# Attention: the order of the three chains in a shared PSUM bank, with the features' chain begun in slot 5 of the batch ahead

## The reference, cut to what matters

```python
x = x + attn_b(layernorm(x), ...)
# attn_b:
q, k, v = split(x @ Wq), split(x @ Wk), split(x @ Wv)
q_amp, k_amp = amp_norm(q), amp_norm(k)   # a = softplus(t); a / sqrt(mean(a*a) + 1e-6)
q_phi, k_phi = pi * tanh(split(x @ Wqp)), pi * tanh(split(x @ Wkp))
scores_phase = (q_amp cos(q_phi)) . (k_amp cos(k_phi)) + (q_amp sin(q_phi)) . (k_amp sin(k_phi))
scores = scale * (q . k) + lam * scale * scores_phase
out = softmax(causal(scores)) @ v
return out.reshape(b, s, d) @ Wo
```

## Time and profile before

| | us |
|---|---|
| median of 3 executions | 1296.38 |
| lowest and highest | 1288.96, 1299.49 |
| profiled execution, its own time | 1298.49 |
| span of the profiled execution | 1296.7 |
| PE busy in the span | 1108.9 (86%) |
| DVE busy | 913.4 (70%) |
| ACT busy | 658.2 (51%) |
| mean granted clock of PE | 0.912 |

### The profile page before, as it was taken

The page is one execution under the profiler, slowest core; times in us unless marked ns, Lnnn a source line. Parts: engine busy times, 40 slices in busy tenths (PEclk is TensorE's granted clock), DMA queues, the critical chain, the costliest instruction groups (busy, mean ns, idle before and its releaser), DMA issues. The chain is left out here.

```text
span 1296.7 us, 16118 instructions
## 1 busy us (share of the span) xinstructions
PE 1108.9 (86%) x5200; PEld 655.8 (51%) x5200; DVE 913.4 (70%) x1933; ACT 658.2 (51%) x1204; POOL 261.1 (20%) x294
## 2 busy tenths in 40 slices
PE   4798888885999999786888888888979968999996
PEld 1222233322666667443455555555556636766774
DVE  2778888884878777675857677675775627787775
ACT  1233333443654555388356565665655646555553
POOL 1444444451000000030122122111212220000000
PEclk9888888886899999888688898998999988999999
DMA  5000000000242322246967568675756302312321
GB/s 189 0 1 1 0 0 0 1 1 1 66 131 66 98 99 66 37 142 169 307 166 203 133 175 204 166 199 136 204 136 148 76 27 105 130 67 81 117 66 65
DMA packets 45502, 129.04 MB, mean 100 GB/s; under 512 B 6512, under 2 KB 8560, under 8 KB 38768
## 3 DMA queue, kind: packets, MB, share of 16 engines
q1 hardware_dynamic: 43376, 127.53, 34.8%
q10 hardware_dynamic: 2048, 0.53, 0.2%
HBM read 88.72 MB, written 36.70 MB: 97 GB/s over the span
## 5 line engine op out<-in xcount | busy, mean ns | idle before, releaser
L1457 DVE TENSOR_REDUCE attn_maxima<-attn_ps_p 128x1 f32<-128x512 f32 (+3 forms) x235 | 146.0, 637 | 101.9 <-PE attn_ps_p L965 87.0
L1834 ACT ACTIVATE moe_hidden<-moe_ps_h 128x512 f32<-128x512 f32 x128 | 76.4, 597 | 147.3 <-PE moe_ps_y L1772 145.7
L1376 POOL TENSOR_SCALAR_AFFINE_SELECT attn_probs<-attn_probs 128x512 f32<-128x512 f32 x128 | 85.1, 700 | 319.0 <-ACT attn_probs L1209 319.0
L960 PE MATMUL attn_ps_p<-attn_stack 96*128 96x384 f32 (+3 forms) x341 | 121.3, 399 | 9.9 <-DVE attn_maxima L1457 9.0
L1956 DVE TENSOR_TENSOR moe_gated<-moe_ps_y,moe_gate_all 128x512 f32<-128x512 f32 x106 | 73.1, 690 | 75.6 <-issue 46.8
L1008 PE MATMUL attn_ps_q<-attn_stack 128*128 128x128 f32 (+3 forms) x343 | 109.7, 384 | 11.3 <-DMA attn_stack<-attn_neg_max 8.6
L1754 PE MATMUL moe_ps_h<-moe_x_high,moe_w_high 128*128 128x512 f32 x256 | 107.5, 420 | 0.0
L1457 DVE TENSOR_REDUCE attn_maxima<-attn_ps_t 128x1 f32<-128x384 f32 (+3 forms) x117 | 74.4, 636 | 45.6 <-PE attn_ps_t L965 43.6
L585 POOL TENSOR_TENSOR rwkv_rs<-rwkv_recept,rwkv_state 128x512 f32<-128x512 f32 x64 | 76.3, 1193 | 136.2 <-DVE rwkv_state L664 132.7
L1756 PE MATMUL moe_ps_h<-moe_x_high,moe_w_low 128*128 128x512 f32 x256 | 103.1, 403 | 0.0
L1755 PE MATMUL moe_ps_h<-moe_x_low,moe_w_high 128*128 128x512 f32 x256 | 102.8, 402 | 0.0
(11 more groups left out here) (256 smaller groups left out, 2452.0 us busy)
## 6 DMA issues: line engine op xcount, KB each, us to landing
moe_gate_all<-moe_gates SPq DMA_DIRECT2D x128, 256.0 KB, 4.9
attn_kept<-attn_parts SPq DMA_DIRECT2D x16, 1536.0 KB, 7.9
attn_stack<-attn_kept SPq DMA_DIRECT2D x64, 384.0 KB
attn_stack<-attn_kept SPq DMA_DIRECT2D x64, 192.0 KB
attn_value<-attn_values SPq DMA_DIRECT2D x5, 1792.0 KB, 12.0
attn_values<-attn_early SPq DMA_DIRECT2D x2, 1792.0 KB, 5.6
attn_values<-attn_probs SPq DMA_DIRECT2D x2, 1792.0 KB, 21.6
experts_in_w<-in_w SPq DMA_DIRECT2D x2, 1024.0 KB, 11.2
```

The costliest lines, as they stand in the source:

```text
L960: return mm(tiles(m)[:, i, :], stack[0][q][0:ROWS, h + i, t * P:(t + 1) * P], stack[1][q][0:ROWS, h + i, 0:(t + 1) * P], **flags)
L1376: nc.gpsimd.affine_select(out=tile, in_=tile, compare_op=ALU.is_ge, fill=0.0, base=0, pattern=[[0, 4], [1, P]], channel_multiplier=-1).the ...
L1457: nc.vector.tensor_reduce(maxima[:, u % 2, h:h + heads, t], tiles, AX_X, ALU.max).then_inc(g_free, 1)
```

## The change

Five things are moved; no instruction of the loop is added or taken away.

- In the bank's order A0 goes from behind FW to behind M0b: from slot 20 to slot 5 of PE. FW goes from slot 17 to 18, E0 from 28 to 29.
- The features of side 0 begin in slot 33 of the batch before (k = -7 in the new numbering), and most other steps get other slots; `high(b, 0, 1)`, for one, goes from slot 25 to 14, and `low(b, 0, 2)` from DVE's slot 31 to 18. For batch 2 these first steps stand ahead of the loop.
- DVE splits the maxima one slot earlier (3, 13, 23, 33 for 4, 14, 24, 34).
- DVE adds FW's product in slot 19 for 18, and normalises E0 in slot 30 for 29.
- SP issues `fetch(b+3)` and `keep(b+2, 0)` ahead of `refill(b, 0, 1)`.

```diff
     for b in range(NB):
         order += [("M0b", b)]
+        order += [("A0", b + 2)] if b + 2 < NB else []
         order += [("E1", b - 1)] if b else []
         order += [("M1a", b)]
         order += [("FT", b - 1), ("FW", b - 1)] if b else []
-        order += [("A0", b + 2)] if b + 2 < NB else []
...
                     refill(b, 0, 0)
-                    refill(b, 0, 1)
                 if b + 3 < NB:
                     fetch(b + 3)
-                if b < LAST:
-                    refill(b, 1, 0)
                 if b + 2 < NB:
                     keep(b + 2, 0)
                 if b < LAST:
+                    refill(b, 0, 1)
+                    refill(b, 1, 0)
                     refill(b, 1, 1)
...  (PE, between)
-                if g == 1 and at == 7 and b:
+                if g == 1 and at == 8 and b:
                     project(b - 1)
-                if g == 2 and at == 0 and b + 2 < NB:
+                if g == 0 and at == 5 and b + 2 < NB:
                     mean("A0", b + 2)
...
-                if at == 8 and g == 2:
+                if at == 9 and g == 2:
                     turn_output("E0", b)
...  (ACT, features; the new list)
+  -7 size 0, -6 exponential 0, -4 log 0, 0 squares 0, 6 log_of_mean 0, 7 inverse 0,
+  8 size 1, 9 high 0 0, 10 exponential 1, 12 log 1, 14 high 0 1, 16 high 0 2, 18 squares 1,
+  20 high 1 0, 26 log_of_mean 1, 27 inverse 1, 34 high 1 1, 36 high 1 2
...  (DVE, features; the new list)
+  -3 softplus 0, 10 amplitude 0, 11 and 12 scale_circle 0, 13 low 0 0, 15 softplus 1,
+  16 low 0 1, 18 low 0 2, 22 low 1 0, 30 amplitude 1, 31 and 32 scale_circle 1,
+  36 low 1 1, 38 low 1 2
...  (ACT and DVE, between, and ahead of the loop)
+                if b + 3 < NB:
+                    features(b + 3, 20 * q + k - 40)
...
+            for k in range(-8, 0):
+                features(2, k)
...  (DVE, between)
-                if at == 4:
+                if at == 3:
                     ... split_maxima
-                if g == 1 and at == 8 and b:
+                if g == 1 and at == 9 and b:
                     add_output(b - 1)
-                if at == 9 and g == 2:
+                if at == 0 and g == 3:
                     normalise("E0", b)
```

More of the change, by code:

```diff
@@ L1236, in features @@
             def features(b, k):
-                if k == 4:
+                if k == -7:
                     size(b, 0)
-                if k == 5:
+                if k == -6:
                     exponential_of_size(b, 0)
+                if k == -4:
+                    log_of_sum(b, 0)
+                if k == 0:
+                    squares(b, 0)
+                if k == 6:
+                    log_of_mean(b, 0)
                 if k == 7:
-                    log_of_sum(b, 0)
+                    inverse(b, 0)
                 if k == 8:
@@ L1245, in features @@
                 if k == 9:
+                    high(b, 0, 0)
+                if k == 10:
                     exponential_of_size(b, 1)
-                if k == 11:
+                if k == 12:
                     log_of_sum(b, 1)
-                if k == 12:
-                    squares(b, 0)
                 if k == 14:
-                    high(b, 0, 0)
+                    high(b, 0, 1)
                 if k == 16:
-                    high(b, 1, 0)
+                    high(b, 0, 2)
                 if k == 18:
                     squares(b, 1)
[L1257 to L1262, removed]
+                if k == 20:
+                    high(b, 1, 0)
                 if k == 26:
@@ L1266, in features @@
                     inverse(b, 1)
-                if k == 29:
-                    high(b, 0, 2)
-                if k == 35:
+                if k == 34:
                     high(b, 1, 1)
-                if k == 37:
+                if k == 36:
                     high(b, 1, 2)
@@ L1487, in features @@
             def features(b, k):
-                if k == 9:
+                if k == -3:
                     softplus(b, 0)
+                if k == 10:
+                    amplitude(b, 0)
+                if k == 11:
+                    scale_circle(b, 0, 1)
+                if k == 12:
+                    scale_circle(b, 0, 2)
                 if k == 13:
+                    low(b, 0, 0)
+                if k == 15:
                     softplus(b, 1)
                 if k == 16:
-                    low(b, 0, 0)
-                if k == 20:
+                    low(b, 0, 1)
+                if k == 18:
+                    low(b, 0, 2)
+                if k == 22:
                     low(b, 1, 0)
[L1496 to L1503, removed]
+                if k == 30:
+                    amplitude(b, 1)
                 if k == 31:
-                    low(b, 0, 2)
+                    scale_circle(b, 1, 1)
                 if k == 32:
[L1507 to L1510, removed]
                     scale_circle(b, 1, 2)
-                if k == 37:
+                if k == 36:
                     low(b, 1, 1)
-                if k == 39:
+                if k == 38:
                     low(b, 1, 2)
```

## The result

The changed kernel took 1288.62 us in the median of 16 runs (1279.4 to 1295.54), the kernel before 1295.68 (1288.88 to 1303.87, 16 runs beside it). The ratio is 0.9937, with a 95% interval of 0.9909 to 0.9964: 7 us faster, where 19 were forecast. By the prediction's own border (1283.4) this counts as no change, to which it gave 0.31. The profiled execution took 1290.17 us, with a span of 1288.4. Its transposes M0b stand at 632.61, 691.31, 743.05, 799.13, 856.43, 909.88, 966.43 and 1009.32 us.

What follows compares the result with a forecast made beforehand. PE sets the pace, though not alone, standing 38.8 us over batches 1 to 5, mostly for the shared bank. Savings of 31.0 - 13.5 - 1.0 + 3.0 = 19.5 us take 1298.5 to 1279.0, or 1277 beside the median; range 1258 to 1297.

Steps and rivals of the forecast that it cites:

- E0: PE's step in slot 28, moved to 29: its wait for a logarithm in ACT's slot 26, 6.3 us, goes whole.
- the prediction's own border: 1283.4 us, the time above which a measurement counts as no change; no change got 0.31, faster 0.60, slower 0.09.
- the second rival: The transfers set the pace: PE stands for late refills in slots 20 or 10, 12 us in all; 1289 us, chance 0.27.
- (a) to (d): PE's shared-bank waits in batches 1 to 5, E0's among them, go whole: 20.7 us saved.
- (e): The wait of E1 for `o_rows` in ACT's slot 6, 2.4 us over batches 1 to 5, shrinks to 1.2.
- E1: PE's step that waited 2.4 us for `o_rows` in ACT's slot 6; 1.2 us expected left.
- (f): PE's waits for DVE's maxima, slots 33 to 38, shrink from 8.2 us to 4.1, the middle of bounds 0 and 8.2.
- (g): PE's waits for the maxima's own DMA shrink from 7.5 us to 2.5 over batches 1 to 5, bounds 0 and 7.5.
- the wait that comes: Slot 30, batches 0 to 5: PE stands 2.7 us each for the refill queued behind the store; 13.5 in batches 1 to 5.
- Moves at no cost: The fetch moved from slot 20 to about 13, and next-batch steps in ACT's slots 33 to 36, cost nothing beyond (g).
- The list of signs: Expected in the new profile: six slot 30 waits for the stack, 2 to 4 us each; if missing, 1261 us.
- The slower rival: Slot 30's stand is 6 us rather than 2.7 and lets PE's clock fall to 0.88: 1313 us, chance 0.09.

Runs made afterwards that it cites:

- compute half alone: The changed kernel with SP's whole order of transfers put back as before; bank order, slots and split stay changed: 1272.98 us, ratio 0.9834.
- transfers spaced: The changed kernel with the refill of slot 19 ahead of side 0's store and the fetch held behind ACT's exponentials of slot 16: 1259.26 us.
- The square: Four kernels with SP's order as before: no edit 1296 us, maxima split earlier 1274.54, steps moved 1285.97, both 1272.98.
- The best kernel: The changed kernel with slot 19's refill ahead of side 0's store and the fetch held behind ACT's slot 16 exponentials: 1259.26 us, ratio 0.9705.
- refill first: The changed kernel with only the refill of slot 19 issued ahead of the store of side 0, nothing held: 1266.14 us, ratio 0.9755.
- late refill: The changed kernel with the fetch held behind ACT's slot 16 exponentials and slot 19's refill, after the store, behind those of slot 26: 1309.48 us.
- the split alone: The kernel before with one edit, DVE splitting the maxima one slot earlier: 1274.54 us, ratio 0.982.
- The pair of batch 5: Batch 5 of the changed kernel (1288.62 us) and of it with the refill ahead of the store, SP's wait for slot 18's low part kept (1263.7 us).

## Why the prediction was partly right and mostly wrong

The direction was right, and 1288.6 lies in the range (1258 to 1297). The size was not: 7 us for 19. The likely cases were ranked wrongly too: the time is that of the second rival (1289), whose place (the refill and the stores' landing, slots 20 and 10) is not where it came from; that it hit the number is luck. The terms over batches 1 to 5, us of PE standing, with the 2.1 us of batch 1 counted to the DMA:

| step | left by forecast | measured |
|---|---|---|
| (a) to (d), waits in the bank | 0 | 0 |
| (e) E1 | 1.2 | 0, and 0.6 of L994 for L1480 |
| (f) DVE's maxima | 4.1 | 10.8 |
| (g) the maxima's DMA in slots 10, 20, 0 | 2.5 | 9.1 |
| the wait that comes, slot 30 | 13.5 | 14.9 |
| sum | 21.3 | 35.4 |

The windows agree: 275.1 us against 278.5 - 17.5 = 261.0, with PE's own busy time all but equal (239.3, and 238.4 before). So two steps failed in about equal parts: the size of (f), 6.7 us too small, and "Moves at no cost", which put the moved `fetch` at nothing though slot 20 then stands 7.9 us; (g) as a whole is 6.6 too small.

**Right.** (a) to (d) went whole, 20.7 us, with no wait of ACT for L1442 left.

**Half right: the wait that comes.** It stands in slot 30, and putting the store behind the refill takes 14.9 us down to 0.4. But it is a wait for the maxima in four of the six batches, 0.6 to 5.2 us, and not one for the stack of 2.7 in each. The list of signs said that without the stack's wait the time would be 1261; it was missing and the time was 1288.6. Batch 0, also put at 2.7 in slot 30, stood 4.0 in slot 20 instead. And 10.7 of the 14.9 stand there with SP's old order too, behind refill and fetch. That the whole of SP's reordering costs 1288.6 - 1273.0 = 15.6 us, for 16.2 forecast, is therefore a coincidence: over batches 1 to 5 it adds 8.7 us of stands (35.8 for 27.1) and 9.3 of PE's own time (239.3 for 230.0).

**Wrong in (g) and in "Moves at no cost".** I took the maxima's DMA to be shortened, since it leaves earlier. Its landing depends on what SP has queued: 2 us, or 6, or 9. I costed the moved transfers only by when their own data is needed, 20 slots of cover for `fetch`, and never asked who else is under way then. With the early fetch slot 20 stands 7.9 us in batches 1 to 4 (2.1, 1.34, 2.10 and 2.33) and 4.0 in batch 0; with the fetch held it stands not at all in batches 1 to 5. None was forecast. In the compute half alone the 2.5 us that (g) leaves in slots 10 and 0 came true, but 10.7 appeared in slot 30, where no term had any. That compute half was forecast at 35.7 us (19.5 + 16.2) and gave 22.7. With the transfers spaced it gives 36.4 (1295.7 - 1259.3), but not by the forecast's terms: DVE's waits alone are 13.8 us there, and 7.1 us of it come from PE's own time (231.3 for 238.4).

**Wrong in (f).** The middle of 0 and 8.2 was taken for want of a row, and 10.8 us came, above the upper bound; the 2 us a batch that the prediction called a sign of being wrong are passed. Per batch it is some 1.5 us ahead of the next M0b, in slots 39 to 1, where softplus and two `low` now end, and 0.57 in the middle of the first unit, behind softplus of side 1. The bound held only the waits of before. The square shows that the moved steps bring these waits, with the split and without it (12.5 and 12.9 against 7.5 and 6.9). Which of them does is read from the places, not shown. The best kernel still has 13.8 us, its largest item. They also trade with other waits: with only the store held, where PE stands for the DMA in slots 20 and 0, they are 5.5.

**The clock, left as it was.** For this kernel that came out, 0.9 us more of PE, but only since two things cancelled: the compute half lowered PE's own time by 8.4 us (230.0 at a granted clock of 0.95), and SP's order took it back. Kernels with the same matmuls spent 239.3 us of PE in batches 1 to 5 at 0.91, 230.5 at 0.95 (refill first) and 240.6 at 0.89 (late refill), with 35.8, 24.5 and 51.2 us of stands. Among these three more stands go with a lower clock, and a kernel with 11.2 us fewer was 20.1 shorter. It isn't a fixed rate: the split alone had 10.4 us fewer stands than the kernel before and 0.8 less of PE, and the kernel before 40.1 of stands with 238.4 of PE at 0.94. The slower rival had a mechanism that exists: the late refill stands 7.4 us in slot 30 of every batch at a clock of 0.89, and came out at 1309.5, on its border of 1309.3.

**The other DMA terms.** The refill was costed at 9.7 us from issue to use, and a run showed 10.3. The Trainium skill, "DMA: Bandwidth & Descriptors", "Anatomy of one DMA", gives a formula by which the estimate is 4.7; the measurement decides against it here. The Trainium skill says on the same page, "Queues, rings and completion order", that one issuing queue's work is taken in ring order. The pair of batch 5 fits: the store lands after 6.9 us when it is first and after 10.8 behind the refill.

**What stays open.** Why the maxima, on a queue of their own, come as late as the refill of SP's queue seems to, and not as late as a store behind it. The Trainium skill says in the section just named that each DMA engine takes turns between the queues, packet by packet, and by that alone a small transfer would be held up little. The Trainium skill also says there that the increment that reports a landing comes only after every earlier write of that engine, across its queues, and this would fit landings that come with the refill's; no run here tells the two apart. Nor is it shown what a store alone, or a load alone of another size, does to them. Nor do the runs settle why the split alone gives 22 us for 8.6 us of waits: in the profiles the loop, from the first M0b to the last, is 14.8 us shorter (369.0 for 383.8), and 5.9 us lie ahead of it, where both kernels have the same instructions.

## What to carry to other kernels

Before moving a large transfer, list the small ones on other queues that leave during it and stand in a chain, and look at their time to landing in the trace. Issue each large transfer right behind such a sending, and the one that is needed first ahead of the others; here the order of two transfers was worth 22.5 us and no bytes were saved. A wait can hide another that ends a little earlier: exchange or hold one transfer at a time to tell them apart. Moving one out of the way of one sending can put it in the way of the next. When a wait is gone, part of the gain may come from the clock.

## What was unexpected of the hardware

- A DMA of maxima, two instructions on ACT's queue, landed in 1.8 to 2.7 us with SP's queue quiet or with only a store issued 5.5 us earlier, in 5.8 to 8.6 behind an early fetch of 1792 KB, and in up to 10.5 behind a store with a refill queued after it. With the same two transfers ahead in the other order it landed in 1.8 to 5.0.
- In the changed kernel it landed 13.0 to 14.8 us after the refill's first issue, whether it was sent 5.1 or 11.6 us after it.
- Issuing on SP got slow right behind a store: the four instructions of the refill took 0.54, 1.11, 1.22 and 1.07 us, 3.9 in all, where such an instruction mostly took 0.31 to 0.39, also with the store issued behind them.
- SP standing for a semaphore ahead of the refill cost nothing that could be measured (1263.7 against 1266.1 us).
- The same matmuls cost PE 230.5 or 239.3 us in five batches, by the granted clock (0.95 and 0.91).
